# Loading the first weight chunk of a cross-attention kernel from two DMA queues instead of one

## The reference

```
q = jnp.einsum('bte,ef->btf', emb, Wq) + bq
k = jnp.einsum('bml,le->bme', latent, Wk) + bk
v = jnp.einsum('bml,le->bme', latent, Wv) + bv
w = jnp.einsum('bte,bme->btm', q, k) * (1 / sqrt(512))
w = jax.nn.softmax(w, axis=1)
pred = jnp.einsum('btm,bme->bte', w, v)
x = pred + emb
out = (x - mean(x)) * rsqrt(var(x) + 1e-6) * gamma + beta
```

## Time and profile before

| | before |
|---|---|
| median of 3 runs | 142.18 us (141.69 to 142.43) |
| the profiled execution's own time | 141.24 us |
| its span (first to last instruction) | 139.4 us |
| granted TensorE clock, mean over the span | 0.995 |
| PE busy | 133.3 us, 96% of the span |
| DVE / ACT / POOL busy | 103.0 / 88.0 / 78.6 us |
| DMA moved | 37.33 MB, mean 268 GB/s |

### The profile page before, as it was taken

The page is one execution under the profiler, slowest core; times in us unless marked ns, Lnnn a source line. Parts: engine busy times, 40 slices in busy tenths (PEclk is TensorE's granted clock), DMA queues, the critical chain, the costliest instruction groups (busy, mean ns, idle before and its releaser), DMA issues.

```text
span 139.4 us, 3004 instructions
## 1 busy us (share of the span) xinstructions
PE 133.3 (96%) x1042; PEld 128.8 (92%) x1042; DVE 103.0 (74%) x208; ACT 88.0 (63%) x299; POOL 78.6 (56%) x77
## 2 busy tenths in 40 slices
PE   7999999999999999999999999999999999999940
PEld 7899999999998999999999999999999999998930
DVE  0789995893545789579696955969596966797983
ACT  4366188989978753988292839565656637386320
POOL 0000005579984695646989272965476553639791
PEclk9999999999999999999999999999999999999997
DMA  4999999984287596978969899599787987535324
GB/s 146 336 397 419 416 260 398 345 302 177 51 292 269 174 360 186 397 258 307 273 266 339 265 333 377 187 356 334 270 252 240 325 277 236 224 111 212 115 75 150
DMA packets 10814, 37.33 MB, mean 268 GB/s; under 512 B 1200, under 2 KB 1456, under 8 KB 10800
## 3 DMA queue, kind: packets, MB, share of 16 engines
q1 hardware_dynamic: 9424, 34.79, 71.6%
q10 hardware_dynamic: 1376, 2.36, 4.6%
HBM read 33.87 MB, written 3.28 MB: 266 GB/s over the span
## 4 chain that ended last, share of the span: by engine, by line
PE 89%; POOL 5%; issue 2%; ACT 1%; POOLq 0%; DVE 0%; DVEq 0%
PE ps_S L427 29%; PE ps_U L441 27%; PE ps_Y L462 10%; PE ps_U L399 6%; PE ps_Y L399 6%; POOL xT_in L990 3%; PE ps_Y L342 2%; POOL xT_in L978 2%; PE ps_w L450 1%; PE ps_S L347 1%; PE ps_U L508 1%; PE ps_c L416 1%; PE ps_U L353 1%; ACT xT_in L626 1%; PE ps_U L358 1%
## 5 line engine op out<-in xcount | busy, mean ns | idle before, releaser
L608 ACT ACTIVATE expo<-scores,negmax 121x100 f32<-121x100 f32 x96 | 34.9, 365 | 22.0 <-DVE negmax L779 22.0
L427 PE MATMUL ps_S<-G,ctxT_in 128*121 128x100 f32 (+1 forms) x384 | 43.3, 269 | 0.0
L427 PEld LDWEIGHTS ps_S<-G,ctxT_in 128*121 128x121 f32 (+1 forms) x384 | 42.1, 185 | 0.0
L441 PEld LDWEIGHTS ps_U<-prob,ctx_in 121*128 121x128 f32 x336 | 39.4, 192 | 1.0
L441 PE MATMUL ps_U<-prob,ctx_in 121*128 121x100 f32 x336 | 39.6, 274 | 0.0
L789 DVE TENSOR_REDUCE probsum<-prob 121x100 f32<-121x600 f32 x16 | 19.8, 1239 | 6.0 <-POOL prob L967 5.7
L978 POOL TENSOR_TENSOR xT_in<-x_in,xT_in 128x512 f32<-128x512 f32 (+1 forms) x13 | 16.6, 1280 | 13.3 <-issue 9.8
L775 DVE TENSOR_TENSOR scores<-ps_S,c_rows 121x600 f32<-121x600 f32 x16 | 12.5, 781 | 15.6 <-issue 12.2
L967 POOL TENSOR_TENSOR prob<-expo,rinv 121x600 f32<-121x600 f32 x16 | 19.0, 1189 | 0.1
L608 ACT ACTIVATION_READ_ACCUMULATOR expo<-scores,negmax 121x1 f32 x96 | 18.0, 187 | 0.0
L990 POOL TENSOR_TENSOR xT_in<-wqk,beta_rows 128x512 f32<-128x512 f32 (+1 forms) x12 | 15.4, 1280 | 2.7 <-ACT wqk L634 2.7
(11 more groups left out here) (125 smaller groups left out, 202.4 us busy)
## 6 DMA issues: line engine op xcount, KB each, us to landing
ctx_in<-ctx SPq DMA_DIRECT2D x16, 768.0 KB, 5.2
ctxT_in<-ctxT SPq DMA_DIRECT2D x16, 722.0 KB, 5.0
xT_in<-xT SPq DMA_DIRECT2D x8, 400.0 KB, 8.7
x_in<-x SPq DMA_DIRECT2D x12, 256.0 KB, 4.5
out<-xT_in ACTq DMA_DIRECT2D x8, 256.0 KB, 3.7
wqk<-Wqk SPq DMA_DIRECT2D x4, 388.0 KB, 4.4
out<-xT_in SPq DMA_DIRECT2D x3, 256.0 KB, 2.0
wv_in<-Wv SPq DMA_DIRECT2D x1, 512.0 KB, 15.5
```

The source lines that it names most:

```text
L427: last = nc.tensor.matmul(ps_scores(c)[0:rows(c), :], ctxT_in[:, q, l * M + c * MP:l * M + c * MP + rows(c)], G[:, l, bass.ds(b * T, T)], ...
L441: last = nc.tensor.matmul(ps_U[:, q, l * T:(l + 1) * T], ctx_in[0:rows(c), q, c, l * P:(l + 1) * P], prob[0:rows(c), q, c * T:(c + 1) * T] ...
L608: last = nc.scalar.activation(expo[0:MP, q, c * T:(c + 1) * T], scores[0:MP, q, c * T:(c + 1) * T], ACT.Exp, bias=negmax[0:MP, q, c:c + 1] ...
```

## The change

The first weight chunk is loaded by two DMAs. SP issues rows 0 to 63 as its first transfer, and ACT issues rows 64 to 127 as its own first instruction, ahead of its wait for the constants. Both add 16 to `w_in[0]`, so the three waits on it (TensorE, ACT, DVE) now ask for 32. Chunks 1 to 3 are loaded as before.

```
@@ sync
-            for c in range(EC):
+            sp.dma_start(wqk[0:P // 2, 0, :], Wqk[0, 0:P // 2]).then_inc(w_in[0], 16)
+            for c in range(1, EC):
                 sp.dma_start(wqk[:, c, :], Wqk[c]).then_inc(w_in[c], 16)
@@ tensor
-            pe.wait_ge(w_in[0], 16)
+            pe.wait_ge(w_in[0], 32)
@@ scalar
+            act.dma_start(wqk[P // 2:P, 0, :], Wqk[0, P // 2:P]).then_inc(w_in[0], 16)
             act.wait_ge(consts_set, 1)
             nc.scalar.activation(ones_r[:, :], ones[:, :], ACT.Copy).then_inc(onesr_set, 1)
             for f in range(EC):
-                act.wait_ge(w_in[f], 16)
+                act.wait_ge(w_in[f], 32 if f == 0 else 16)
@@ vector
-                dve.wait_ge(w_in[c], 16)
+                dve.wait_ge(w_in[c], 32 if c == 0 else 16)
```

## The result

| | before | after |
|---|---|---|
| median (14 runs each) | 141.75 us (140.71 to 142.43) | 143.53 us (lowest 141.53) |
| ratio of the undisturbed runs | | 1.0071, 95% interval 1.0038 to 1.0103 |
| profiled execution, its span | 141.24, 139.4 us | 143.76, 141.9 us |

The change makes the kernel slower. The runs after it fall into a group of 4 at 141.53 to 142.28 us and a group of 9 at 143.47 to 144.05, and the ratio understates the loss, because it leaves out every run more than 1.5% above the fastest of its kernel, five of the upper group among them. By the medians the loss is 1.8 us, 1.3%. One further run took 764.8 us; no trace of it exists and its cause is open.

What follows compares the result with a forecast made beforehand. TensorE was taken to bound the kernel (89% of the chain). ACT's issue 0, SP's 0, chunk 0's landing 0 to -0.1, given back later; 142.18 less 0.05 to 0.1 gives 142.1 us, range 141.6 to 142.9.

Steps and rivals of the forecast that it cites:

- rival B: ACT's half lands late, behind or between chunk 1's packets, TensorE idles: +0.5 to +1.0 us, up to 0.4 more; chance 0.14.
- The reading of the bottleneck: TensorE is 89% of the chain, which starts on it; its early shifts can reach the end unless another engine holds it.
- ACT's part: ACT's new DMA issues in 0.56 us, table load ends at 2.57, 1.1 us of cover left before chunk 0: cost 0.
- chunk 0's landing: First weight chunk lands between 0.5 us earlier and 0.63 later; middle taken, 3.9 to 4.0 as now, perhaps 0.1 earlier.
- where I took 0: SP's first transfer with half the rows: 0.2 us saved if issue time went by rows, but bytes limit landing, so 0.
- the price of idle TensorE time: In rival B: the start's shift, plus up to 0.4 us if two more fp32 products run at 1.2 GHz.
- The rule of the page: Skill says "Don't bother" splitting by partition halves, same 16 DMA engines; by it alone the landing stays, sum 0.

Runs made afterwards that it cites:

- e9: Kernel before with chunk 0 split into two column halves (128 rows, 388 columns each), both issued by SP; 142.10 us, ratio 1.0039.
- the second profile: The changed kernel run once more, unchanged, for another profile; 143.50 us, span 141.7 us.
- e7: Changed kernel with chunk 0 split by columns in place of rows, one half on SP, one on ACT; 141.81 us, ratio 0.9990.
- e3: Changed kernel with 9 warm-up matmuls instead of 7; 142.11 us, ratio to before 1.0023.
- e4: Kernel before with 5 warm-up matmuls instead of 7; 143.35 us, ratio 1.0098.
- e11: Kernel before with 9 warm-up matmuls instead of 7; 142.00 us, ratio 1.0016.
- e5: Changed kernel with chunk 0's rows dealt out differently, even rows on SP and odd rows on ACT; 142.19 us, ratio 1.0029.
- e10: Kernel before, chunk 0 whole on SP, with ACT issuing 128 rows of x (tile 1) first; 142.58 us, ratio 1.0071.
- e6: Kernel before, chunk 0 whole on SP, with ACT issuing the first 64 rows of x first; 142.93 us, ratio 1.0100.
- e1: Changed kernel with both 64-row halves of chunk 0 issued by SP; 143.79 us, ratio 1.0128.

## Why the prediction was wrong

The forecast was 142.1 and no shift; it was 143.5. What came is the case of rival B, which had 0.14: ACT's half is late and TensorE idles. Its reasons weren't borne out. B had ACT's packets behind or between those of chunk 1, but hardly more bytes had moved at the landing than before (0.70 and 0.67 MB), and the split of columns over the same two queues was hardly late (4.14). Its price fell short as well: it is a loss of at most 1.0 + 0.4 = 1.4 us, and 1.8 were lost. That 143.5 stands within B's numbers is luck, since they start from 142.18, the median of three runs of before, and the 14 runs have 141.75.

**The reading of the bottleneck held.** TensorE leads the chain, the loss of 2.46 us at the projection is at the end undiminished, and an earlier landing bought nothing (e9). ACT's part held too: issue 0.59 for 0.56, its table load ends at 2.65 for 2.57, and 1.78 us of waiting are left.

**The step that failed first is chunk 0's landing**, "so the landing lies between 0.5 us earlier and 0.63 later", with the middle taken because both issues start together. It came 0.77 later, and 1.0 in the second profile. The sum rested on the issue times, and the one row for ACT was misread: 559 ns for ACT's first store was taken as the price of being first. That store is also the only one with 64 rows (tile 0), and the other eight have 128. In e7 ACT's first transfer has 128 rows and took 0.41, while its store of tile 0, no longer the first, took:

```profile
L640 ACTq DMA_DIRECT2D out<-xT_in x1: 544/544/544, 52.1 to 52.1; - x1
```

So the row said that 64 rows cost about 0.2 more to issue, and the same came on SP, where I took 0 ("Whether 64 rows issue faster no row says"). With 64 rows at the head of SP's queue the first packets start at 2.06 to 2.08 in all five profiles that have them, and at 1.73 to 1.76 in the other eight. That is 0.3 of the 0.77 us. The other 0.4 to 0.5 are lost in the lower rate from 2.75 to 3.75, which stays unexplained.

**The step that cost most is the price of idle TensorE time.** B was priced at the shift of the start plus "up to 0.4 more" for the 1.2 GHz level. Idle time at the lower level is worth 1.4 to 1.5 us (after against e3, e4 against before), and what is left of the loss once the gap is closed is 0.3 (e3). The rows to see it were there: the earlier trace rows with 770 falling to 381 says that the rise came during these four products, hardly a microsecond after the warm-up's end, so a gap in front of them was a gap before the rise. I counted the products that ran slowly in before, and not those that would run slowly if the rise failed to come.

**The rule of the page.** The Trainium skill, "DMA: Bandwidth & Descriptors", section "Rules for kernel authors", advises against two transfers to partition halves since both use the same engines. The runs agree with the advice (1.0071 for this change, 1.0128 with both halves on SP). They go past its reason, which says that nothing is gained and not that something is lost.

The start on chunk 0 is 0.7 to 1.0 us later in the profiles after the change and in e3, yet e3 loses only 0.3 in the medians. Part of that is that the profiled execution of before, at 141.24, is 0.5 us faster than the median of all its runs: the shown 10.68 for the projection was a good one. That the forecast was set against the median and not against this execution was right.

## What to carry to other kernels

Look first at what follows the warm-up. If data can come late there, the price is not the delay but the time that TensorE then stays on the lower level, here 1.4 us by the medians for a gap of 1.03. Two more dummy matmuls removed that (e3, no run of 12 in the upper group), and where no gap had been they cost about 0.3 us, little more than the noise (e11). If a first load has to be split, split it by columns and keep 128 rows in each transfer, which here lost nothing and gained nothing (e7). And compare the issue time of a row with the shape of its transfer, not only with its place in the queue.

## What the runs showed of the hardware that I had not expected

- A first load of 64 rows takes 0.56 to 0.60 us to issue, one of 128 rows at the same place 0.37 to 0.41, on SP and ACT. On SP the 128-row load right behind it takes 0.56 to 0.58 too (five profiles). ACT's store of 64 rows takes 0.52 to 0.57, its stores of 128 rows mostly 0.34. With 64 rows at the head of both queues, or of SP's alone, the first packets start 0.3 us later.
- Of the kernels whose profile shows 0.41 us of idle time or less, 1 run of 60 took 143.2 us or more, of e5 (0.73) 1 of 12, of those with 1.03 and more 32 of 54 (without the 764.8). It doesn't grow steadily with the idle time: after (1.03) has 9 of 13, e10 (1.16) 3 of 10 and e6 (1.47) 5 of 12.
- TensorE's granted clock rose while the engine stood idle in e1 and e6 (4.47 and 4.80 us), and not before 6.90 in e11, where it had not been idle since its first warm-up matmul.
- TensorE's level at the start doesn't show in the clock column or the busy shares of the views; it shows in the time from one matmul of known width to the next (0.215 or 0.12 us for 258 columns).
- A second queue with other bytes at the start (e6, e10) delayed chunk 0 by 0.9 to 1.2 us, more than its bytes explain; two queues with a column half each (e7) by less than 0.2. Open.
